# Eight transformer parts on one core: a third of the unweighed scores of the first attention get their log weights from VectorE, and the feed-forwards 1 and 3 are rearranged

## The chip, the cores and the metric

The kernel runs on one core of a Trainium2 chip, as one launch. A core has TensorE (PE: matmul; PEld: its weight loads), VectorE (DVE), ScalarE (ACT), GpSimd (POOL) and SyncE (SP, which issues transfers). Each engine works through its own list of instructions in order, and waits on counting semaphores. The metric is the device time in microseconds, median of some runs.

## The reference

The reference is a chain of eight parts on x of 2 x 1024 tokens with 128 values each; before every part x is normalised (layer norm), and the part's result is added to x. The change touches three places: the scores of the first attention, the first feed-forward and the third one (the parts l0_attn, l0_ffn, l2_ffn of the kernel).

```python
# first attention: 16 heads of 8 values, weight 1/(distance+1) for earlier keys, none for later ones
delta = pos[None, :] - pos[:, None]
log_d = jnp.log(jnp.maximum(delta, 0).astype(jnp.float32) + 1.0)
mask = jnp.where(delta > 0, (-ALPHA * log_d).astype(dtype), jnp.zeros((), dtype))
mask = jnp.where(delta < 0, jnp.asarray(-jnp.inf, dtype), mask)
scores = jnp.einsum('bhqd,bhkd->bhqk', q, k) * scaling
scores = scores + _power_law_mask(S, scores.dtype)[None, None]
attn = jax.nn.softmax(scores, axis=-1)
# first feed-forward: three int32 weights of 384 x 128, times 1/127
h = jax.nn.silu(gate) * up
return jnp.einsum('bsh,dh->bsd', h, wd)
# third feed-forward: 8 experts, each token weighs two of them; every expert is run on all tokens
h = jax.nn.gelu(jnp.einsum('td,edf->etf', xt, w1) + b1[:, None, :], approximate=False)
o = jnp.einsum('etf,efd->etd', h, w2) + b2[:, None, :]
y = _layernorm(xt[None, :, :] + o, ln_g[:, None, :], ln_b[:, None, :])
out = jnp.einsum('et,etd->td', wE, y)
```

## The kernel before

The tokens are 16 tiles of 128, or 4 chunks of 512 (`NC`, `CH`). The parts run one after the other; every engine's list holds all parts, and semaphores join them.

**First attention.** There are 8 units (batch, group of 4 heads). Of each unit 12 groups (512 or fewer queries by 128 keys) are scored; a group has two halves (`p`), and a half is two heads, so there are 192 halves of 2 x 512, 384, 256 or 128 scores. `scores_by_key` (L498 to L524) computes a half into two PSUM banks; the halves' banks go round over three banks (`BANK`), so PE can be one and a half halves ahead, and `free_bank` makes it wait until the bank that it takes next is read. ACT takes the exponential from PSUM to SBUF (`exp`, L606). The weight 1/(distance+1) comes in by one of two ways: for the 133 halves in `BY_POOL`, POOL multiplies the exponentials (`weigh`, L420); for the 59 others PE adds the logarithm to the scores in PSUM, as a high and a low part, by two matmuls with an identity for each head (L518, L519). `times_v` (L540) multiplies by the values up to three groups later. At the same time PE scores the next unit by query in "pieces" (L475, L481, L487), of which DVE takes the row maxima (L671); `split_maxima` (L682 to L690) and `turn_maxima` (L495) make them ready for the next unit, and `divide` (L698, L701) finishes 512 queries. `schedule` writes out one order for all of this, by due positions (one for each half, 24 in a unit), and each engine picks its own steps from it in that order. In unit 0 the pieces come ahead of everything, and unit 7 has none beside it.

**First feed-forward** (`l0_ffn`). For each chunk `wait_xnT` transposes the normalised x on PE (L152) one chunk ahead, ACT copies it to SBUF (L165), PE multiplies it by the gate and the up weights, three times 2 matmuls of 512 columns in float32 (L757), ACT takes silu (L781), DVE multiplies (L795) and so frees the pair of banks (two pairs), and after the next chunk's gates PE multiplies down (`down`, L766). DVE converts the int32 weights (L747) before its last normalisation, and PE waits for that. `add` and `after` on DVE add the result to x (L787) and begin the next norm (L94, L98, L106); POOL computes the reciprocal root (L117, L119).

**Third feed-forward** (`l2_ffn`). There are 8 experts times 4 chunks, 32 steps `n`. In a step PE runs `up(n)` (12 matmuls: w1 and x are split into high and low parts, L1384 to L1386) and `down(n-1)` (L1397, L1402). The weights of expert e+1 are made ready during expert e: ACT rounds w1 to its high part (L1440), POOL subtracts for the low part (L1484) and centres w2 (L1489) with a mean that DVE computes (L1520, L1522). ACT also takes the squares of the sums (L1453), from which POOL computes the scales of each step (L1498, L1500, L1504) for DVE (L1580). The same splitting of x, on ACT (L168) and POOL (L125), is done at the beginning of this part.

## Time and profile before

| what | value |
|---|---|
| median of 3 runs | 1120.84 us (1120.64 to 1128.33) |
| the profiled execution | 1129.11 us, span 1127.3 us |
| mean granted TensorE clock of the span | 0.891 of full speed (full is 2.4 GHz, half is 1.2 GHz) |
| PE busy | 908.3 us, 81% of the span |
| DVE / POOL / ACT busy | 646.1 / 510.8 / 429.1 us |

The busy shares are means over eight parts with different limits, so the parts must be read one by one. The span less the median is 6.5 us: the profiled execution is one of the longer ones.

### The profile page before, as it was taken

How to read it: one execution, taken by the hardware profiler on the slowest of the kernel's cores; microseconds unless marked ns; L12 is line 12 of the kernel's file. 1: busy time of each engine (PE TensorE's matmuls, PEld its weight loads, DVE VectorE, ACT ScalarE, POOL GpSimd, SP SyncE). 2: the span in 40 equal slices, each digit the busy share in tenths (PEclk: the TensorE clock that was granted, in tenths of full speed). 3: DMA queues.
4: the chain of work that ended last, by engine and by line, in shares of the span. 5: the costliest groups of instructions: out<-in, count | busy, mean ns of one | idle time of the engine just before them, and what ended most of it. 6: DMA issues, size and time to landing. Idle time of an engine off the chain costs nothing. (4 is left out here: it accounts for less than half of the span.)

```text
span 1127.3 us, 17905 instructions
## 1 busy us (share of the span) xinstructions
PE 908.3 (81%) x6590; PEld 612.6 (54%) x6590; DVE 646.1 (57%) x1445; ACT 429.1 (38%) x1018; POOL 510.8 (45%) x458
## 2 busy tenths in 40 slices
PE   4558999999998878267899789995998996398983
PEld 2113333333433446154566678885895766388883
DVE  6757676767670155979687556778103666542324
ACT  2324664665556421014111365674344211032221
POOL 4335978897888611052322344554200001156561
PEclk9658999999998988758799599998899998599997
DMA  4800110011000000001000000121100000266664
GB/s 156 238 1 2 29 31 13 18 30 30 3 1 23 1 22 8 0 15 39 1 2 2 10 10 19 46 95 33 43 1 1 1 10 28 77 199 207 201 205 137
DMA packets 38747, 55.95 MB, mean 50 GB/s; under 512 B 6682, under 2 KB 26146, under 8 KB 38534
## 3 DMA queue, kind: packets, MB, share of 16 engines
q1 hardware_dynamic: 36166, 49.70, 14.9%
q0 software_dynamic: 2496, 5.12, 1.4%
q8 instruction: 54, 0.88, 0.3%
q14 instruction: 31, 0.25, 0.1%
HBM read 43.66 MB, written 10.94 MB: 48 GB/s over the span
## 5 line engine op out<-in xcount | busy, mean ns | idle before, releaser
L671 DVE TENSOR_REDUCE arena<-ps 128x2 f32<-128x1024 f32 (+2 forms) x192 | 177.6, 956 | 87.6 <-PE ps L487 55.4
L420 POOL TENSOR_TENSOR arena<-arena 128x1024 f32<-128x1024 f32 (+3 forms) x105 | 201.2, 1957 | 37.9 <-ACT arena L606 37.8
L606 ACT ACTIVATE arena<-ps 128x512 f32<-128x512 f32 (+3 forms) x320 | 138.6, 489 | 89.4 <-PE ps L519 56.2
L117 POOL TENSOR_SCALAR vareps<-meanvar 128x4 f32<-128x4 f32 x32 | 8.0, 251 | 236.2 <-DVE meanvar L98 236.2
L511 PE MATMUL ps<-arena 51*128 51x512 bf16 (+3 forms) x384 | 91.0, 342 | 18.1 <-ACT arena L606 6.8
L511 PEld LDWEIGHTS ps<-arena 51*128 51x128 bf16 x384 | 27.0, 94 | 105.0 <-ACT arena L606 58.6
L2076 PE MATMUL ps<-arena 128*128 128x128 f32 x624 | 78.2, 280 | 0.0
L152 PE MATMUL ps<-ident,xn 128*128 128x128 f32 x128 | 26.4, 356 | 62.1 <-DVE x L922 19.9
L2076 PEld LDWEIGHTS ps<-arena 128*128 128x128 f32 x624 | 74.7, 196 | 0.0
L420 POOL TENSOR_TENSOR xnT<-xnT,arena 128x1024 f32<-128x1024 f32 (+1 forms) x28 | 52.7, 1902 | 40.5 <-ACT xnT L606 40.5
L487 PE MATMUL ps<-arena 48*128 48x512 bf16 (+3 forms) x320 | 56.8, 351 | 16.8 <-DVE arena L671 14.1
L540 PE MATMUL ps<-arena 128*9 128x512 f32 (+3 forms) x640 | 66.6, 492 | 0.0
L2242 DVE TENSOR_TENSOR arena<-ps,arena 128x512 f32<-128x512 f32 x39 | 27.0, 692 | 66.0 <-PE ps L2076 34.7
L1402 PEld LDWEIGHTS ps<-arena 128*128 128x128 f32 x512 | 63.0, 194 | 2.9
L1402 PE MATMUL ps<-arena 128*128 128x128 f32 x512 | 62.9, 276 | 0.0
L165 ACT ACTIVATE xnT<-ps 128x512 f32<-128x512 f32 x32 | 18.9, 596 | 114.3 <-PE ps L152 107.4
L2036 POOL DMA_INDIRECT expert_rows<-arena x39 | 38.6, 990 | 47.6 <-ACT arena L2124 44.5
L152 PEld LDWEIGHTS ps<-ident,xn 128*128 128x128 f32 x128 | 20.0, 186 | 66.0 <-issue 40.7
L2023 POOL DMA_INDIRECT arena<-token_rows,arena x39 | 38.1, 976 | 36.9 <-DVEq L2224 24.7
L1453 ACT ACTIVATE arena<-arena 128x128 f32<-128x128 f32 x128 | 38.0, 298 | 35.8 <-DVE arena L1571 35.8
L1267 DVE TENSOR_TENSOR arena<-ps,arena 128x512 f32<-128x512 f32 x64 | 39.7, 682 | 17.6 <-PE ps L1149 17.6
L2110 ACT ACTIVATE arena<-ps 128x512 f32<-128x512 f32 x39 | 23.3, 597 | 68.1 <-PE ps L2076 58.3
(340 smaller groups left out, 2034.4 us busy)
## 6 DMA issues: line engine op xcount, KB each, us to landing
arena<-in_L_ffn_w SPq DMA_DIRECT2D x39, 512.0 KB
arena<-scratch SPq DMA_DIRECT2D x32, 192.0 KB, 4.0
arena<-in_L_ffn_w SPq DMA_DIRECT2D x16, 256.0 KB, 3.3
scratch<-arena SPq DMA_DIRECT2D x12, 256.0 KB, 4.0
arena<-expert_rows SPq DMA_DIRECT2D x8, 256.0 KB, 4.7
scratch<-arena SPq DMA_DIRECT2D x4, 384.0 KB, 5.7
scratch<-arena SPq DMA_DIRECT2D x12, 128.0 KB, 4.2
x<-in_x SPq DMA_DIRECT2D x4, 256.0 KB, 3.9
```

The costliest lines, as they stand in the source:

```text
L152: last = nc.tensor.transpose(m.ps[:, self.banks[n % len(self.banks)], j * P:(j + 1) * P], m.xn[:, n * TPC + j, :], m.ident[:, :])
L420: nc.gpsimd.tensor_tensor(e, e, weight[:, at:at + k].unsqueeze(1).broadcast_to([P, 2, k]), ALU.mult).then_inc(weighed, 1)
L487: mm = nc.tensor.matmul(m.ps[:, bank + e, 0:wd], qs[rows, u % BUFS, pair, at * P:(at + 1) * P], ks[rows, u % BUFS, pair, j:j + wd], start= ...
L511: mm = nc.tensor.matmul(m.ps[:, bank, 0:wd], ks[rows, u % BUFS, p, kt * P:(kt + 1) * P], qs[rows, u % BUFS, p, CH * qc:CH * qc + wd], star ...
L540: mm = nc.tensor.matmul(m.ps[PAD * h:PAD * h + HD + 1, 7, 0:wd], vones[:, b * TB + kt, u % G * GH + h, :], probs(u * NG + n)[:, h, 0:wd], ...
L606: nc.scalar.activation(probs(g)[:, 2 * p + e, 0:wd], m.ps[:, BANK[h, e], 0:wd], ACT.Exp, scale=SCALE).then_inc(exps, 1)
L671: nc.vector.tensor_reduce(out, scores, AX.X, ALU.max, negate=True).then_inc(max_set, 1)
L1267: nc.vector.tensor_tensor(at[:, t % 2, g, :].rearrange("p (j q) -> p j q", q=P), m.ps[:, g, :].rearrange("p (j q) -> p j q", q=P), causal[ ...
L1402: mm = nc.tensor.matmul(m.ps[:, 4 + n % 2, j * P:(j + 1) * P], hT[:, n % 2, f, j * P:(j + 1) * P], w2c[:, e % 2, f, :], start=False, stop= ...
L2023: nc.gpsimd.indirect_dma_start(xg[:, s % RING, :], None, m.token_rows, bass.IndirectOffsetOnAxis(ap=token_i[:, s:s + 1], axis=0),).then_in ...
L2036: nc.gpsimd.indirect_dma_start(m.expert_rows, bass.IndirectOffsetOnAxis(ap=target_i[:, s:s + 1], axis=0), y[:, s % RING, :], None,).then_i ...
L2076: mm = nc.tensor.matmul(m.ps[:, 2 * (s % 2) + half, f * P:(f + 1) * P], w_up[:, s % WBUFS, at + f * P:at + (f + 1) * P], xgT[:, s % 2, :], ...
```

## The change

- **First attention.** `shares` also picks a third (by columns) of the halves that POOL doesn't weigh, `BY_VECTOR`: 21 halves, of which 8 have 512 columns for each head, 1 has 384, 3 have 256 and 9 have 128. For these PE adds nothing (`with_log` is false); DVE adds the logarithm (`add_logs`) from PSUM into the SBUF buffer of the exponentials, in one instruction where the two banks are neighbours and in two where they aren't, and so frees the banks; ACT then takes the exponential of both heads in place by one instruction (`exp_log`), one position later in the schedule, ahead of the next half's. The 8 wide halves are those of position 8 in each unit.
- **First feed-forward.** x is split into a high and a low part as in the third one (a second copy on ACT, a subtraction on POOL), and the 24 float32 matmuls for gate and up become 48 in float32r. The int32 weights are converted by ACT after the attention's last copy, in two instructions, with the scale moved to silu and to the down weights.
- **Third feed-forward.** Rounding, subtraction, centring and mean of the next expert's weights come at its predecessor's first chunk (`c == 0`) instead of the second; on ACT ahead of the squares and on POOL ahead of the step's scales.
- The second attention's buffers are laid behind the area of the split x, with no other change.

```diff
...
@@ -295,9 +295,14 @@
             if pool + (1500 if diagonal(n) else 0) <= gone:
                 by_pool.add(h)
                 pool += 80 + 2.25 * k
-        return by_pool
-
-    BY_POOL = shares()
+            else:
+                others += k
+                if vector + k / 2 <= others / 3:
+                    by_vector.add(h)
+                    vector += k
+        return by_pool, by_vector
+
+    BY_POOL, BY_VECTOR = shares()
     POOL_COUNT = list(itertools.accumulate(h in BY_POOL for h in range(UNITS * HALVES)))
     def schedule():
@@ -309,7 +314,11 @@
             for n in range(NG):
                 for p in range(2):
                     at = 2 * (u * NG + n) + p
-                    due.setdefault(at, []).append(("exp", u, (n, p)))
+                    if at in BY_VECTOR:
+                        due.setdefault(at, []).append(("log", u, (n, p)))
+                        due.setdefault(at + 1, []).append(("exp_log", u, (n, p)))
+                    else:
+                        due.setdefault(at, []).append(("exp", u, (n, p)))
         for at, pieces in PIECES_AT.items():
             due[at] += [("max", u, n) for u, n in pieces]
         for u in range(UNITS):
...
@@ -342,11 +351,21 @@
             BANK[job] = 4 + k % 3
         freed = {}
         for what, u, n in schedule():
-            h = u * HALVES + 2 * n[0] + n[1] if what == "exp" else None
+            h = u * HALVES + 2 * n[0] + n[1] if what in ("exp", "log", "exp_log") else None
             if what == "exp":
                 for e in range(2):
                     counts[exps] += 1
                     freed[h, e] = (exps, counts[exps])
+                EXPS[h] = counts[exps]
+            if what == "log":
+                for e in range(2):
+                    counts[logged] += 1 if e or BANK[h, 1] != BANK[h, 0] + 1 else 0
+                    freed[h, e] = (logged, counts[logged])
+                if BANK[h, 1] == BANK[h, 0] + 1:
+                    freed[h, 0] = freed[h, 1]
+                LOGGED[h] = counts[logged]
+            if what == "exp_log":
+                counts[exps] += 1
                 EXPS[h] = counts[exps]
             if what == "turn_max":
                 freed[what, u, n] = (mrows_set, u + 1)
@@ -503,7 +522,7 @@
                 pe.wait_ge(mrows_in[u % BUFS], 16 * GH * (u // BUFS + 1))
             wd = width(n)
             with_mask = h in BY_POOL and diagonal(n)
-            with_log = h not in BY_POOL
+            with_log = h not in BY_POOL and h not in BY_VECTOR
             off = weight_at(n)
             for e in range(2):
                 rows = slice(HALF * e, HALF * e + LONG)
...
@@ -605,6 +624,13 @@
                 act.wait_ge(s_mm, 2 * h + e + 1)
                 nc.scalar.activation(probs(g)[:, 2 * p + e, 0:wd], m.ps[:, BANK[h, e], 0:wd], ACT.Exp, scale=SCALE).then_inc(exps, 1)
+        def exp_of_logged(u, at):
+            n, p = at
+            g = u * NG + n
+            ps = probs(g)[:, 2 * p:2 * p + 2, 0:width(n)]
+            act.wait_ge(logged, LOGGED[2 * g + p])
+            nc.scalar.activation(ps, ps, ACT.Exp, scale=SCALE).then_inc(exps, 1)
+
         def take_numerators(u, qc):
             k = u * QC + qc
...
@@ -701,7 +727,25 @@
             nc.vector.tensor_tensor(o[:, t0:t0 + TPC, g * GH * HD:(g + 1) * GH * HD].rearrange("p t (h e) -> p t h e", e=HD),
                                     turned[:, :, :, 0:HD], r.unsqueeze(3).broadcast_to([P, TPC, GH, HD]), ALU.mult).then_inc(o_set, 1)
-        do = {"max": maximum, "split": split_maxima, "divide": divide}
+        def add_logs(u, at):
+            n, p = at
+            g = u * NG + n
+            h = 2 * g + p
+            k = width(n)
+            off = weight_at(n)
+            if g >= RING:
+                dve.wait_ge(pv_mm, g - RING + 1)
+            dve.wait_ge(log_steps, 5)
+            if BANK[h, 1] == BANK[h, 0] + 1:
+                dve.wait_ge(s_mm, 2 * h + 2)
+                nc.vector.tensor_tensor(probs(g)[:, 2 * p:2 * p + 2, 0:k], m.ps[:, BANK[h, 0]:BANK[h, 0] + 2, 0:k],
+                                        logw[:, off:off + k].unsqueeze(1).broadcast_to([P, 2, k]), ALU.add).then_inc(logged, 1)
+            else:
+                for e in range(2):
+                    dve.wait_ge(s_mm, 2 * h + e + 1)
+                    nc.vector.tensor_tensor(probs(g)[:, 2 * p + e, 0:k], m.ps[:, BANK[h, e], 0:k], logw[:, off:off + k], ALU.add).then_inc(logged, 1)
+
+        do = {"max": maximum, "split": split_maxima, "log": add_logs, "divide": divide}
         for what, u, n in schedule():
             if what in do:
                 do[what](u, n)
@@ -726,15 +770,20 @@
 def l0_ffn(nc, m, A, sem, sb, norm):
+
+
     F = 384
     FT = F // P
     SCALE = 1.0 / 127.0
+    m.rounded.fresh()
+    x_high, x_low = norm.split_xnT()
+    w_up = m.rounded.take("l0f_w_up", [P, 2, F], F32R)
     wi = sb("l0f_wi", [P, 3, F], I32)
-    w = sb("l0f_w", [P, 3, F])
+    w_down = sb("l0f_w_down", [P, F])
     sg = sb("l0f_sg", [P, 2, CH])
     hT = sb("l0f_hT", [P, 2, FT, CH])
     w_in, w_all = norm.loads(1)
-    w_scaled = sem("l0f_w_scaled")
+    w_set = sem("l0f_w_set")
     up_done = sem("l0f_up_done")
     sg_done, h_done = sem("l0f_sg_done"), sem("l0f_h_done")
     down_done, x_done = sem("l0f_down_done"), m.x_done
@@ -742,20 +791,23 @@
     def sync(sp):
         sp.dma_start(wi[:, :, :], A["L0_ffn_w"]).then_inc(w_in, 16)
-    def dequantise(dve):
-        dve.wait_ge(w_in, w_all)
-        nc.vector.tensor_scalar(w[:, :, :], wi[:, :, :], SCALE, None, ALU.mult).then_inc(w_scaled, 1)
+    def widen(act):
+        act.wait_ge(w_in, w_all)
+        nc.scalar.activation(w_up[:, :, :], wi[:, 0:2, :], ACT.Copy).then_inc(w_set, 1)
+        nc.scalar.activation(w_down[:, :], wi[:, 2, :], ACT.Copy, scale=SCALE * SCALE).then_inc(w_set, 1)
     def tensor(pe):
         def gates(c):
             norm.wait_xnT(pe, c)
+            cs = slice(c * CH, (c + 1) * CH)
             for f in range(FT):
                 s = c * FT + f
                 if s >= 2:
                     pe.wait_ge(h_done, s - 1)
                 for half in range(2):
-                    nc.tensor.matmul(m.ps[:, 2 * (s % 2) + half, :], w[:, half, f * P:(f + 1) * P], m.xnT[:, c * CH:(c + 1) * CH],
-                                     start=True, stop=True).then_inc(up_done, 1)
+                    out, lhsT = m.ps[:, 2 * (s % 2) + half, :], w_up[:, half, f * P:(f + 1) * P]
+                    nc.tensor.matmul(out, lhsT, x_high[:, cs], start=True, stop=False)
+                    nc.tensor.matmul(out, lhsT, x_low[:, cs], start=False, stop=True).then_inc(up_done, 1)
         def down(c):
             if c >= 2:
...
@@ -778,7 +830,7 @@
         for s in range(NC * FT):
             norm.copy_xnT(act, s // FT + 1)
             act.wait_ge(up_done, 2 * s + 1)
-            nc.scalar.activation(sg[:, s % 2, :], m.ps[:, 2 * (s % 2), :], ACT.Silu).then_inc(sg_done, 1)
+            nc.scalar.activation(sg[:, s % 2, :], m.ps[:, 2 * (s % 2), :], ACT.Silu, scale=SCALE).then_inc(sg_done, 1)
     def vector(dve, after):
         def add(c):
@@ -798,14 +850,14 @@
         add(NC - 1)
     return Part([(x_done, norm.done(c)) for c in range(NC)], tensor=tensor, vector=vector, scalar=scalar, sync=sync,
-                before_norm={"vector": dequantise})
-
+                before_norm={"scalar": widen})
 def l1_attn(nc, m, A, sem, sb, norm):
     H, HD = 16, 8
     HB = NT // 2
     SCALE = HD ** -0.5
+    sb("rounded", [P, 2 * T + 2 * 384])
     wqk = sb("l1a_wqk", [P, 2, D])
     rope = sb("l1a_rope", [P, P])
     w = sb("l1a_w", [P, 5, D])
@@ -1468,12 +1520,12 @@
                 act.wait_ge(step, 2 + RANK_STEPS)
                 nc.scalar.activation(gap[:, :], gap[:, :], ACT.Exp).then_inc(exps, 1)
             if n == 4:
-                for c in range(NC):
-                    turn(c)
+                for k in range(NC):
+                    turn(k)
+            if c == 0 and e + 1 < E:
+                round_weights(e + 1)
             if n:
                 squares(n - 1)
-            if c == 1 and e + 1 < E:
-                round_weights(e + 1)
         squares(STEPS - 1)
     def gpsimd(pool):
@@ -1492,6 +1544,8 @@
         split_weights(0)
         for n in range(STEPS):
             e, c = divmod(n, NC)
+            if c == 0 and e + 1 < E:
+                split_weights(e + 1)
             if n >= 4:
                 pool.wait_ge(y_set, n - 3)
             pool.wait_ge(squared, n + 1)
@@ -1502,8 +1556,6 @@
             if n == 0:
                 pool.wait_ge(wte_set, 1)
             nc.gpsimd.tensor_tensor(wrs[:, n % 4, :], rs[:, n % 4, :], wte[:, c * TPC:(c + 1) * TPC, e], ALU.mult).then_inc(scales, 1)
-            if c == 1 and e + 1 < E:
-                split_weights(e + 1)
     def vector(dve, after):
         count = [0]
@@ -1603,7 +1655,7 @@
                 for k in range(NC):
                     add_biases(k)
                 dve.wait_ge(lnb_added, NC)
-            if c == 1 and e + 1 < E:
+            if c == 0 and e + 1 < E:
                 sum_weights(e + 1)
         for n in (STEPS - 2, STEPS - 1):
             add(n)
```

PE at position 8 of one unit of the first attention, before: the half's scores (L511), its four log matmuls (L518, L519), a piece (L475, L481), and the next half's scores.

```order
L540 MATMUL ps<-xnT,arena 9x512 x4
L511 MATMUL ps<-arena 128x512 x2
L518 MATMUL ps<-rounded 128x512
L519 MATMUL ps<-rounded 128x512
L518 MATMUL ps<-rounded 128x512
L519 MATMUL ps<-rounded 128x512
L475 MATMUL ps<-arena 128x512 x2
L481 MATMUL ps<-arena 128x128 x8
L511 MATMUL ps<-arena 128x512 x2
```

The same place now (L530 are the scores, L494 and L500 the piece):

```order
L559 MATMUL ps<-xnT,arena 9x512 x4
L530 MATMUL ps<-arena 128x512 x2
L494 MATMUL ps<-arena 128x512 x2
L500 MATMUL ps<-arena 128x128 x8
L530 MATMUL ps<-arena 128x512 x2
```

The four log matmuls are gone, so the piece and the next half's scores follow at once. On DVE the same place was, before, a `divide` and then maxima:

```order
L698 RECIPROCAL arena<-ps 128x16 [waits l0a_num_turned]
L701 TENSOR_TENSOR xn<-ps,arena 128x4x32 [waits l0a_rec_set]
L671 TENSOR_REDUCE arena<-ps 128x2x4 [waits l0a_a_mm]
L671 TENSOR_REDUCE arena<-ps 128x2 [waits l0a_a_mm] x6
```

and is now (L746 are the two additions, L697 the maxima):

```order
L724 RECIPROCAL arena<-ps 128x16 [waits l0a_num_turned]
L727 TENSOR_TENSOR xn<-ps,arena 128x4x32 [waits l0a_rec_set]
L746 TENSOR_TENSOR arena<-ps,arena 128x512 [waits l0a_s_mm,l0a_log_steps,l0a_pv_mm]
L746 TENSOR_TENSOR arena<-ps,arena 128x512 [waits l0a_s_mm]
L697 TENSOR_REDUCE arena<-ps 128x2x4 [waits l0a_a_mm]
L697 TENSOR_REDUCE arena<-ps 128x2 [waits l0a_a_mm] x6
```

Two additions stand ahead of the piece's maximum. POOL in the third feed-forward, before: the scales of a step (L1498, L1500, L1504), then the weights of the next expert (L1484, L1489), which stood behind the scales of the second chunk.

```order
L1498 TENSOR_SCALAR arena<-arena 128x4 [waits l2f_squared,l2f_y_set]
L1500 TENSOR_TENSOR arena<-arena,power 128x4 [waits l2f_scales]
L1504 TENSOR_TENSOR arena<-arena 128x4 [waits l2f_scales]
L1484 TENSOR_TENSOR rounded<-arena,rounded 128x256 [waits l2f_up_done,l2f_w1_high_set]
L1489 TENSOR_SCALAR arena<-arena 128x128 [waits l2f_o_done,l2f_w2_summed]
L1489 TENSOR_SCALAR arena<-arena 128x128
```

Now (L1536 and L1541 are the weights, L1552, L1554 and L1558 the scales) they stand ahead of the scales of the first chunk:

```order
L1536 TENSOR_TENSOR rounded<-arena,rounded 128x256 [waits l2f_up_done,l2f_w1_high_set]
L1541 TENSOR_SCALAR arena<-arena 128x128 [waits l2f_o_done,l2f_w2_summed]
L1541 TENSOR_SCALAR arena<-arena 128x128
L1552 TENSOR_SCALAR arena<-arena 128x4 [waits l2f_squared,l2f_y_set]
L1554 TENSOR_TENSOR arena<-arena,power 128x4 [waits l2f_scales]
L1558 TENSOR_TENSOR arena<-arena 128x4 [waits l2f_scales]
```

The block has moved up by the scales of two steps.

## Rows read from the trace of the kernel before

**Rows 1.** Busy time by stretch: us, PE, PEld, DVE, ACT, POOL, clock, DMA.

```profile
72.00:384.00 312.00, 285.93 (x2186) 111.40 (x2187) 186.29 (x238) 178.29 (x406) 251.56 (x132) 0.95 0.06 16
252.00:288.00 36.00, 33.32 (x279) 12.85 (x278) 25.43 (x34) 21.27 (x50) 29.36 (x17) 1.00 0.08 23
402.00:439.00 37.00, 36.52 (x160) 22.90 (x160) 16.83 (x51) 10.84 (x17) 3.21 (x6) 0.92 0.03 6
```

**Rows 2.** Waits in the first attention (80 to 395): us, times, longest.

```profile
PEld ps L511 <- ACT arena L606: 58.6, 126, 0.9
PEld ps L487 <- DVE arena L671: 15.3, 26, 1.4
PEld ps L540 <- POOL arena L420: 0.8, 5, 0.2
```

**Rows 3.** Groups of instructions by shape in the same stretch.

```profile
L606 ACT ACTIVATE arena<-ps 128x512 f32<-128x512 f32 x158 | 84.6, 597 | 43.3 <-PE ps L519 29.9 <-PE ps L511 7.1 <-PE ps L523 6.3
L671 DVE TENSOR_REDUCE arena<-ps 128x2 f32<-128x1024 f32 x55 | 67.1, 1224 | 24.6 <-PE ps L487 24.4
L671 DVE TENSOR_REDUCE arena<-ps 128x2 f32<-128x512 f32 x28 | 19.3, 691 | 10.3 <-PE ps L487 10.3
```

**Rows 4.** Timeline at position 8 of unit 4: start, us, what.

```profile
245.52 4.71 POOL L420 TENSOR_TENSOR arena<-arena 128x1024 f32<-128x1024 f32 x2
246.25 0.29 DVE L701 TENSOR_TENSOR xn<-ps,arena 128x128 f32<-128x128 f32 x1
246.28 0.39 PE L511 MATMUL ps<-arena 51*128 51x512 bf16 x2
246.60 0.50 PE L518 MATMUL ps<-rounded 128*128 128x512 f32 x1
247.63 0.60 PE L475 MATMUL ps<-arena 128*128 128x512 bf16 x2
248.40 0.38 PE L511 MATMUL ps<-arena 51*128 51x512 bf16 x2
249.04 1.08 ACT L606 ACTIVATE arena<-ps 128x512 f32<-128x512 f32 x2 [0.54 <-PE ps L523]
```

**Rows 5.** Timeline at position 14 of unit 5, DVE beside POOL.

```profile
294.28 3.11 DVE L682 TENSOR_TENSOR arena<-arena 128x28 f32<-128x28 f32 x2
294.61 2.52 POOL L420 TENSOR_TENSOR xnT<-xnT,arena 128x512 f32<-128x512 f32 x2
```

**Rows 6.** Timeline of the first feed-forward.

```profile
400.58 1.31 POOL L119 TENSOR_TENSOR rstd<-vareps,power 128x4 f32<-128x4 f32 x1
401.90 1.97 PE L152 MATMUL ps<-ident,xn 128*128 128x128 f32 x8 [5.80 <-DVE arena L747]
403.70 7.50 PE L757 MATMUL ps<-xnT,arena 128*128 128x512 f32 x12
411.48 5.32 PE L757 MATMUL ps<-xnT,arena 128*128 128x512 f32 x12
416.63 2.84 PE L766 MATMUL ps<-arena 128*128 128x128 f32 x24
```

**Rows 7.** Groups that split x, at the beginning of the third feed-forward.

```profile
L125 POOL TENSOR_TENSOR rounded<-xnT,rounded 128x512 fp32r<-128x512 f32 x4 | 5.2, 1305 | 6.4 <-ACT rounded L168 6.4
L168 ACT ACTIVATE rounded<-xnT 128x512 fp32r<-128x512 f32 x4 | 2.5, 630 | 0.1
```

**Rows 8.** Third feed-forward: its wait, and the timeline at a new expert.

```profile
PEld ps L1384 <- POOL rounded L1484: 9.7, 6, 2.1
704.11 0.48 PE L1384 MATMUL ps<-rounded 128*128 128x512 f32 x1
707.51 0.48 PE L1384 MATMUL ps<-rounded 128*128 128x512 f32 x1
712.48 0.50 PE L1384 MATMUL ps<-rounded 128*128 128x512 f32 x1 [1.33 <-POOL rounded L1484]
711.70 0.73 POOL L1484 TENSOR_TENSOR rounded<-arena,rounded 128x256 fp32r<-128x256 f32 x1
```

16 lines of the change are left out of this document (8 added, 8 removed).

## The prediction

> **What bounds the kernel now.** I read the busy times by stretch first. In the first attention PE is busy 285.93 of 312 us, POOL 251.56, DVE 186.29 and ACT 178.29; in its middle PE is busy 33.32 of 36 us at full clock [rows 1]. So PE comes first, POOL has about a fifth to spare, DVE two fifths. The waits say what PE's rest is: it waits for ACT to read a bank, 126 times and 58.6 us by the weight loads, never over 0.9 us; it waits for DVE's maxima 26 times, 15.3 us; for POOL's weighing 0.8 us [rows 2]. That is a PE with a short leash: three banks let it run one and a half halves ahead of the exponentials. Work taken from PE is therefore a gain only as far as ACT and the banks keep up. In the first feed-forward PE is busy 36.52 of 37 us [rows 1], so it is the bound alone. In the third, the wait to look at is that of an expert's first matmul for POOL's low part of the weights: six times, 9.7 us, 2.1 at most [rows 8].
>
> **First attention.** For 21 of 59 halves the log matmuls go. At 512 columns the four of them hold PE from 246.60 to 247.63, 1.03 us [rows 4]. The 21 halves have 8 x 512 + 384 + 3 x 256 + 9 x 128 = 6400 columns a head; by columns that is 6400 / 512 x 1.03 = 12.9 us of PE, the most that this part can give (a little more, since narrow ones have a fixed share).
>
> What it adds is DVE's. No row has an addition of a PSUM tile and an SBUF row of this size; the maximum of 512 columns from PSUM takes 691 ns and of 1024 takes 1224 [rows 3], and I take the same: 6400 x 2 / 1024 x 1.22 = 15 us, some 17 with the fixed parts. DVE goes from 186 to 203 of 312 and stays no bound. What counts is latency. I walk through position 8, which is in each unit and has 512 columns. The scores start at 246.28 and are there 0.39 later, at 246.67; DVE has finished with L701 at 246.54 [rows 4] and is free. Its additions end near 247.4 and 248.1 (the order shows two of them, each frees its bank). PE does the piece at once: it took from 247.63 to 248.40, 0.77 us [rows 4], so the next scores could start at 246.60 + 0.77 = 247.4 instead of 248.40. So far a gain of 1.0. But ACT now waits for 248.1, and then takes both heads in one instruction, about 1.05 us (two of 597 ns [rows 3], less one start), to 249.15. Before, it began the next half at 249.04 [rows 4]. So ACT gains nothing, and PE two halves on needs a bank that ACT reads until 249.15 + 0.6 = 249.75. Before, PE got there at 249.04 + 1.08 = 250.1 or a little later, as the half's second exponential was done. What is left is 0.4 to 0.5 of the 1.0. I take 0.5 for each of the 8 wide halves: 4 us.
>
> Of the 13 narrower halves PE loses at least 2304 / 512 x 1.03 = 4.6 us of work. Some stand at positions 22 and 23, right after a maximum that DVE is still at, and two at position 15, behind `split_maxima`, whose first two instructions took 3.11 us there [rows 5]: the additions queue behind it, then ACT's exponential of that half, and behind that its next one, while PE has to wait for the same maxima anyway. One at position 14 of unit 0 goes the other way: `split_maxima` stands behind the additions and so waits for scores that it did not need. I take plus 1.5 for those that lie well and minus 1.5 for these: nothing. Sum for the attention: 4 us. Ends: 13 if PE stays the bound everywhere; 4 us slower if each of the 21 costs a maximum's length on ACT's path (1.22) where PE is given 0.6 to 1.03.
>
> POOL's work is the same; at 251.56 of some 308 it is still not the bound. Its first instructions of a unit run back to back, but the multiplication by v comes three groups later, and the 0.8 us in [rows 2] say how seldom that is late.
>
> **A rule of the skill on DVE's additions.** While POOL ran without a pause (245.52 to 250.23), DVE's L701, one input from PSUM and one from SBUF, took 0.29 us [rows 4]. DVE's L682, both inputs in SBUF and only 28 columns, took 3.11 us for two, and ended with POOL's two instructions (297.39 against 297.13) [rows 5]. The Trainium skill (SBUF — State Buffer, section "SBUF: two separate sides") says that POOL and a VectorE instruction with two SBUF inputs take a shared pair of ports as an exclusive lock; by that rule the additions, with one input in PSUM, are free of it, and the trace agrees. It is the rival below if it is otherwise.
>
> **First feed-forward.** At the beginning PE no longer waits for the int32 conversion (5.80 us idle, released by L747) [rows 6]. But its first gates now wait for the first x_low. POOL is at the reciprocal roots until 400.58 + 1.31 = 401.89 [rows 6], and a subtraction takes 1.305 [rows 7]: 403.2, against 403.70 [rows 6]. Gain 0.5. The two conversions on ACT lie in its idle time ahead of this. The gates of the first chunk took 7.50 us, mostly at half clock; the next chunk's took 5.15 (411.48 to 416.63) [rows 6]. A float32r matmul costs 1.03 / 4 = 0.26 [rows 4], 12 for a chunk 3.1; at half clock up to 6.2, by most of the chunk at half clock 5.7. First chunk: gain 0.5 + 1.8 = 2.3. The other three: 5.15 - 3.1 = 2.05 each, less a new stall. Two pairs of banks: the third product waits for DVE's multiplication of the first, 1.03 + 0.60 + 0.69 + signals = 2.4 after the start, where PE could start it at 2.06; and while a chunk is being copied ahead, ACT does two copies of 0.60 and 0.63 [rows 3, 7] before its first silu. That is 0.3 to 1.3 a chunk; I take 1.0. Gain 3 x 1.05 + 2.3 = 5.4; I take 5. The down matmuls (2.84) [rows 6] stay and give the chain time. Ends: 2, if the stall takes all of the 2.05; 9, if there is none.
>
> **Third feed-forward.** A step takes 707.51 - 704.11 = 3.40 us, but that into a new expert 712.48 - 707.51 = 4.97 [rows 8]: 1.57 more, and POOL's L1484, from 711.70 for 0.73, releases it. Five such and one of 2.1 are the 9.7. The block moves up by the scales of two steps, 6.8 us, against a lateness of 1.6; L1484 then ends some 5 us before PE wants it. What is late next? Its inputs: ACT rounds after the first chunk's gelus, three steps ahead. DVE's mean comes two steps before the need. The block on POOL, 2.0 us, now stands in front of the first chunk's scales, for which POOL also waits until DVE has the mean; DVE uses these scales two steps later, so I put it at 0.2 in all. The next load from DRAM starts earlier too, and is waited for nowhere. Gain 9.5; ends 8 and 10.
>
> **Sum.** 4 + 5 + 9.5 = 18.5 us. The profiled execution has 1129.1 (a span of 1127.3 and 1.8 around it) and would have 1110.6. It is 8.3 above the median of the runs shown, and nothing of the sum hangs on that; against the median, 1120.8 - 18.5 = 1102.3.
>
> **Rivals.**
> - *PE is the bound throughout the attention.* The 33.32 of 36 speaks for it, the 126 waits for ACT against. 13 instead of 4: 1093.
> - *The attention gives nothing.* DVE's additions come late behind maxima, ACT's list stands still behind them, and the banks stay full: the leash decides. For it: the 58.6 us of waits. With 0 to 3 us lost there and 2 to 5 in the first feed-forward: 1120.8 - 9.5 - 3.5 + 1.5 = 1109.
> - *The clock falls.* PE's mean clock over the stage is 0.95 [rows 1]. Another 5% of it at half clock, 16 us, would cost up to 8: 1110. Against it: the middle of the stage has many short waits already and runs at 1.00 [rows 1]. The Trainium skill (TensorE: Matmul & The Clock Gate, section "A second HAM failure mode: psum-queue depth-cycling") warns that frequent short idle times while PE cycles through banks make the clock change between its levels; the trace doesn't show that here.
> - *The additions are held up by POOL*, as L682 was. Then each of the 21 halves waits for one POOL instruction at least, 4.71 / 2 = 2.36 [rows 4], and ACT, the banks and PE behind it: 50 us, 1120.8 + 50 - 14.5 = 1156. It decides from 0.9 us a half on (14.5 + 4 over 21). L701 speaks against it.
>
> **How the numbers follow.** Forecast 0.55 (its own range 1097 to 1107), PE bound 0.12, nothing from the attention 0.22, clock 0.07, held up 0.04. A measurement of this kernel can tell about 1% from no change, 11 us: 1109.6. The forecast, the PE case, most of the third and half of the clock's lie below it: 0.83 faster, 0.13 the same, 0.04 slower. The range runs from the PE case to the clock's: 1091 to 1112.
>
> **What the profile will show.** PE's wait for L1484's successor gone, and the 32 steps 3.40 us apart (if not: the third part of the sum is wrong). Additions of 0.69 or 1.22 us while POOL is busy (if 2 or more: held up). ACT waiting for DVE at its exponentials in place, and PE's waits for ACT grown while its log matmuls shrink by 84; the stage near 308 us. In the first feed-forward 48 matmuls 0.26 apart, PE idle about 1 us a chunk, and the part 5 us shorter. Wrong would be, above all, an attention that is no shorter, or gains in it over 8 us.

## The result

The changed kernel takes 1116.7 us, the median of 20 runs (1107.9 to 1122.2). The kernel before, run beside it, takes 1127.3 (20 runs, 1120.0 to 1131.7), not the 1120.8 of the three runs shown before. The ratio is 0.991, with a 95% interval of 0.989 to 0.993: 10.6 us faster, where 18.5 were forecast. The means of the experiments below take in all runs; without those that took over 1.5% longer than the fastest of their kernel (three of e6, one of e8, three of e11), these three kernels stand 3.1, 23.4 and 23.9 us below the kernel before instead of -0.1, 21.6 and 18.2, and no reading below hangs on the difference.

From the two profiles I took the times at which the stages begin and end (first scores of the first attention, its last addition to x, first matmul of the second attention that reads x, first matmul with w1 of the third feed-forward, its last addition to x).

| stage | before | after | forecast |
|---|---|---|---|
| first attention | 325.9 | 333.9 | -4 |
| from there to the second attention | 48.2 | 41.5 | -5 |
| second attention and what follows | 194.0 | 194.1 | 0 |
| third feed-forward | 143.3 | 133.7 | -9.5 |
| from there to the end, not edited | 343.0 | 339.2 | 0 |

The two feed-forwards gave 6.7 and 9.6 us, as forecast; the attention, for which a gain of 4 was forecast, lost 8.0. Its busy times, and the lines of the same view around one place in unit 4 (the columns are those of [rows 1]):

```profile
72.00:384.00 312.00, 279.53 (x2074) 98.75 (x2074) 204.35 (x271) 173.57 (x376) 247.26 (x129) 0.92 0.06 16
...
254.40:257.60 3.20, 2.98 (x30) 0.96 (x26) 3.17 (x2) 0.89 (x4) 3.20 (x4) 1.00 0.00 0
257.60:260.70 3.10, 1.41 (x18) 0.75 (x14) 2.59 (x7) 0.68 (x1) 0.34 (x1) 1.00 0.00 0
260.70:264.10 3.40, 3.40 (x24) 0.91 (x22) 2.24 (x2) 2.37 (x5) 2.04 (x1) 0.50 0.04 10
```

DVE went from 186.29 us to 204.35, as forecast (203). But the granted clock of the stage fell from 0.95 to 0.92. The last three lines show such a fall: PE is busy 2.98 of 3.20 us at full clock (2.4 GHz), then only 1.41 of 3.10, and the next 3.40 us are granted at 0.50 (1.2 GHz). The stage (to its last addition) has 59.0 us at the half clock, against 29.0 before. Two of the stage's falls, at 260.7 and at 342.6, begin 1.3 and 2.3 us behind the end of a gap of over 1.1 us in which PE waits for the same line; two more such gaps, ending at 221.73 and 300.08, have no fall within 11 us. The timeline shows whose the gap at 259.37 is:

```profile
254.54 3.64 DVE L708 TENSOR_TENSOR arena<-arena 128x28 f32<-128x28 f32 x2
255.31 1.26 POOL L439 TENSOR_TENSOR xnT<-xnT,arena 128x512 f32<-128x512 f32 x1
256.53 1.41 POOL L439 TENSOR_TENSOR arena<-arena 128x256 f32<-128x256 f32 x2
259.02 0.30 DVE L716 TENSOR_TENSOR arena<-arena 128x32 bf16<-128x32 f32 x1
259.37 0.61 PE L514 MATMUL ps<-arena 128*12 128x128 bf16 x8 [1.69 <-DVE arena L716]
260.02 1.01 ACT L645 ACTIVATE arena<-ps 12x1024 bf16<-12x1024 bf16 x1 [3.59 <-PE ps L514]
```

`split_maxima` (L708, 28 columns, both inputs in SBUF) starts at 254.54 and its two instructions end at 258.2, just after POOL's weighing has stopped at 257.94. PE waits for the end of the split to turn the maxima. The groups by shape say what such an instruction takes on average, and what an addition takes:

```profile
L708 DVE TENSOR_TENSOR arena<-arena 128x28 f32<-128x28 f32 x7 | 16.4, 2349 | 0.2
L746 DVE TENSOR_TENSOR arena<-ps,arena 128x512 f32<-128x512 f32 x16 | 10.3, 686 | 3.4 <-PE ps L530 3.4
```

The additions take 0.69 us, as the maxima of the same width do [rows 3], while POOL runs. The Trainium skill (SBUF — State Buffer, section "SBUF: two separate sides") says that POOL and a VectorE instruction with two SBUF inputs exclude each other; the trace agrees for both kinds.

The waits of the same stretch:

```profile
PEld ps L530 <- ACT arena L625: 55.7, 114, 1.5
...
ACT arena L632 <- DVE arena L746: 27.3, 12, 4.0
...
PEld ps L514 <- DVE arena L716: 13.1, 7, 2.6
```

PE's wait for ACT is what it was (58.6 us, 126 times [rows 2]), though 84 log matmuls are gone; ACT now waits for additions, up to 4 us; and PE waits longer for the split's last line than it did in the kernel before:

```profile
PEld ps L495 <- DVE arena L690: 8.9, 6, 2.5
```

In the first feed-forward the gates start 4.14 us after the last addition to x (405.95) instead of 4.84:

```profile
408.68 2.49 POOL L125 TENSOR_TENSOR rounded<-xnT,rounded 128x512 fp32r<-128x512 f32 x2
408.74 3.03 DVE L106 TENSOR_SCALAR xn<-x,meanvar,rstd 128x128 f32<-128x128 f32 x4 [0.47 <-POOL rstd L119]
410.09 0.76 PE L809 MATMUL ps<-rounded 128*128 128x512 f32 x1 [2.98 <-POOL rounded L125]
414.87 0.60 PE L152 MATMUL ps<-ident,xn 128*128 128x128 f32 x4
415.23 0.48 PE L809 MATMUL ps<-rounded 128*128 128x512 f32 x1
419.14 2.84 PE L818 MATMUL ps<-arena 128*128 128x128 f32 x24
```

The first chunk's gates take 5.14 us (410.09 to 415.23), mostly at half clock, where 7.78 were taken (403.70 to 411.48 [rows 6]); the second chunk's take 3.91 (to 419.14) instead of 5.15. In the third feed-forward the steps into experts 3 to 7 are 3.40 us apart like those around them, and no wait for POOL's low part (now L1536) is left; only among the first nine steps are there longer ones, up to 10.70 us, as before (10.15):

```profile
701.48 0.48 PE L1436 MATMUL ps<-rounded 128*128 128x512 f32 x1
702.27 0.74 POOL L1536 TENSOR_TENSOR rounded<-arena,rounded 128x256 fp32r<-128x256 f32 x1
704.88 0.48 PE L1436 MATMUL ps<-rounded 128*128 128x512 f32 x1
```

### The profile page after: what moved, and what is told of

It is laid out like the page before. It is cut to its first block and busy times, and to the rows that moved or that the text cites. A ratio compares the mean times of both kernels' runs of the same rounds, so it can differ in the third digit from the quotient of the medians.

```text
span 1114.5 us, 17760 instructions
## 1 busy us (share of the span) xinstructions
PE 898.0 (81%) x6506; PEld 603.8 (54%) x6506; DVE 666.1 (60%) x1477; ACT 429.0 (38%) x1003; POOL 511.9 (46%) x462
## 5 line engine op out<-in xcount | busy, mean ns | idle before, releaser
L697 DVE TENSOR_REDUCE arena<-ps 128x2 f32<-128x1024 f32 (+2 forms) x192 | 177.3, 954 | 69.4 <-PE ps L506 49.7
L625 ACT ACTIVATE arena<-ps 128x512 f32<-128x512 f32 (+3 forms) x278 | 122.8, 499 | 58.3 <-PE ps L538 29.4
L530 PE MATMUL ps<-arena 51*128 51x512 bf16 (+3 forms) x384 | 96.2, 352 | 23.4 <-ACT arena L625 8.7
L530 PEld LDWEIGHTS ps<-arena 51*128 51x128 bf16 x384 | 28.2, 95 | 118.9 <-ACT arena L625 56.0
L559 PE MATMUL ps<-arena 128*9 128x512 f32 (+3 forms) x640 | 73.8, 540 | 0.0
L2088 POOL DMA_INDIRECT expert_rows<-arena x39 | 38.5, 987 | 41.2 <-ACT arena L2176 40.6
L152 PEld LDWEIGHTS ps<-ident,xn 128*128 128x128 f32 x128 | 18.9, 177 | 63.6 <-issue 43.3
```

The lines of the kernel that those rows point to most:

```text
L152: last = nc.tensor.transpose(m.ps[:, self.banks[n % len(self.banks)], j * P:(j + 1) * P], m.xn[:, n * TPC + j, :], m.ident[:, :])
L530: mm = nc.tensor.matmul(m.ps[:, bank, 0:wd], ks[rows, u % BUFS, p, kt * P:(kt + 1) * P], qs[rows, u % BUFS, p, CH * qc:CH * qc + wd], star ...
L559: mm = nc.tensor.matmul(m.ps[PAD * h:PAD * h + HD + 1, 7, 0:wd], vones[:, b * TB + kt, u % G * GH + h, :], probs(u * NG + n)[:, h, 0:wd], ...
L625: nc.scalar.activation(probs(g)[:, 2 * p + e, 0:wd], m.ps[:, BANK[h, e], 0:wd], ACT.Exp, scale=SCALE).then_inc(exps, 1)
L697: nc.vector.tensor_reduce(out, scores, AX.X, ALU.max, negate=True).then_inc(max_set, 1)
L2088: nc.gpsimd.indirect_dma_start(m.expert_rows, bass.IndirectOffsetOnAxis(ap=target_i[:, s:s + 1], axis=0), y[:, s % RING, :], None,).then_i ...
```

## The experiments

Three theories stand behind the expectations. **L** (the lock): `split_maxima` is held up by POOL, and the additions make that worse. **C** (the clock): with its log matmuls gone TensorE has too little to do, and its clock is taken down. **B** (banks and ACT's order): the additions hold banks, and ACT's list stands still behind them.

The runs are in three groups (e1 to e4, e5 to e8, e9 to e12), each on one chip with the kernel before beside them; before took 1127.1, 1133.9 and 1132.3 us (medians of 16 or 17). So kernels of different groups are compared by their distance to before, in means of all their runs; differences are taken before rounding. The changed kernel's own 20 runs are a fourth group, in which before's clock is known for the profiled run only; 0.894 is taken for it. "Clock" is the mean granted clock of these whole runs (before: 0.894, 0.891, 0.894). Within a kernel, the runs with a lower clock are the longer ones: over all 157 runs, with a level of its own for each kernel and group, by 6.8 us for each 0.01. "At one clock" is the distance with both sides brought to 0.890 by that slope. It is an estimate: taken kernel by kernel, the slope lies anywhere from 1.8 to 10.5 us. "Attention" is the profiled stage, with its half-clock time.

| kernel | log matmuls of the 21 halves | DVE's additions | POOL's wait | less than before, us | clock | at one clock | attention (half clock) |
|---|---|---|---|---|---|---|---|
| before | yes | no | no | 0 | 0.894 | 0 | 325.9 (29.0) |
| changed | no | yes | no | 10.2 | 0.878 | 21.2 | 333.9 (59.0) |
| e1, attention alone | no | yes | no | -4.9 | 0.884 | 2.3 | 334.9 (62.0) |
| e2, feed-forwards alone | yes | no | no | 19.0 | 0.891 | 21.1 | 332.3 (45.6) |
| e3 | no | yes | yes | 18.0 | 0.878 | 28.9 | 327.2 (65.8) |
| e4 | yes | no | yes | 25.7 | 0.894 | 25.9 | 318.5 (21.5) |
| e12, e4 again | yes | no | yes | 26.3 | 0.895 | 25.9 | 324.6 (38.5) |
| e5 | dead, ahead | yes | yes | 14.1 | 0.893 | 12.6 | 332.0 (28.4) |
| e6 | dead, ahead | yes | no | -0.1 | 0.878 | 8.9 | 344.9 (61.9) |
| e7 | all but at position 8 | at position 8 | yes | 24.3 | 0.888 | 26.5 | 320.1 (34.4) |
| e8 | at position 8 | elsewhere | yes | 21.6 | 0.883 | 27.2 | 324.7 (48.6) |
| e9 | no; as much dead work with V, behind | yes | yes | 2.9 | 0.886 | 8.6 | 343.6 (53.5) |
| e10 | no | no, unweighed | yes | 36.8 | 0.890 | 39.5 | 311.1 (38.3) |
| e11 | all but at 8 to 15 | at 8 to 15 | yes | 18.2 | 0.882 | 26.5 | 317.2 (27.4) |

**e1 and e2: the two parts of the change apart.** e1 is the kernel before with the attention's part of the diff, e2 with the feed-forwards' parts.

> The kernel before with the attention's part of the change alone. My prediction's sum had 4 us of gain for it. What the profile after suggests instead is a loss: from the first scores to the last addition to x it is 8 us longer. Theory L (the shared lock): the additions lie ahead of the maxima on DVE and shift DVE against POOL, so that the first instruction of the split of the maxima (both inputs in SBUF) starts where POOL works without a pause, and is held longer; PE stands for it once a unit. Theory C (the clock): PE has 84 matmuls fewer, stands more often, and falls to half clock. Theory B (banks and ACT's order alone): ACT waits for the additions. All three expect 3 to 10 us slower than before here. L expects the mean of the 28-column instruction over 2 us (1.57 before); C more than 30 us at half clock in the stage (10 before); B ACT's waits for the additions to end PE's waits, with no change in the split.

> The kernel before with the changes of the first and third feed-forward alone, the attention as before. My sum had 5 + 9.5 = 14.5 us; the profile after shows 6.7 + 9.6 = 16. If the parts add up, 15 to 17 us faster than before, and faster than the changed kernel by 4 to 8. If the attention's part is worth the 4 us that I forecast and something else is wrong, this kernel is slower than the changed one.

e1: 1131.1 us, ratio 1.004 (1.002 to 1.006). e2: 1109.2, ratio 0.984 (0.981 to 0.988). The attention's part alone makes the kernel slower, by 4 to 5 us; put upon e2 it costs 8.8 (19.0 to 10.2). The feed-forwards give 19.0, more than the 15 to 17 expected: the third gained 12.4 us in e2's profile, 9.6 in the changed kernel's. (The "10 before" of half clock in the expectation of e1 leaves out the start of the stage; the whole stage has the 29.0 of the table.)

**e3 and e4: POOL pauses for the split.** POOL waits once a unit, before its first weighing from position 12 on, for the split of the next unit's maxima; e3 is the changed kernel with it, e4 is e2 with it.

```
+    if u + 1 < UNITS and waited == u and 2 * n + p >= 12:
+        pool.wait_ge(nparts_set, u + 2)
+        waited = u + 1
```

> The changed kernel, but POOL waits once in each unit, ahead of its first weighing from position 12 on, until DVE has split the maxima (a wait for nparts_set). Nothing is left out. Theory L: DVE's first split instruction is no longer held, its mean falls from 2.35 us to under 0.8, PE's wait for the split (13.1 us in seven units) falls to under 6, and the kernel is 4 to 10 us faster than the changed one; POOL has the time, since it pauses for 3 us right after. Theory C alone: half clock as often, time within 2 us of the changed kernel. Theory B: no gain, or a loss from POOL's later weighing.

> The kernel with the two feed-forward changes and the attention as before, with the same wait of POOL for the split of the maxima. Theory L: the split was held before the change too (1.57 us in the mean for 28 columns), so this gains 2 to 6 us over the kernel without the wait, and is the fastest of the four. If the lock isn't what holds it, no change, or slower by POOL's pause.

e3: 1108.0, ratio 0.985 (0.982 to 0.988). e4: 1100.5, ratio 0.978 (0.975 to 0.981), faster than both kernels. The split's first instruction, in e3, e4 and e2 in this order:

```profile
L712 DVE TENSOR_TENSOR arena<-arena 128x28 f32<-128x28 f32 x7 | 4.3, 621 | 0.2
```
```profile
L686 DVE TENSOR_TENSOR arena<-arena 128x28 f32<-128x28 f32 x7 | 3.3, 477 | 0.2
```
```profile
L682 DVE TENSOR_TENSOR arena<-arena 128x28 f32<-128x28 f32 x7 | 15.4, 2201 | 0.2
```

That the split waits for POOL is real and is worth 7 us, but it is worth nearly as much without the additions (19.0 to 25.7, 6.7 us) as with them (10.2 to 18.0, 7.8). It is an old cost of this kernel (1574 ns in the profile of before) and not what the change lost. Theory L falls as the cause. With the split free, the additions still cost 7.7 us.

**e5, e6 and e9: TensorE gets its work back.** If the loss is that TensorE has too little to do and its clock is taken down, dead work must bring it back. In e5 and e6 the four log matmuls are issued ahead of the half's scores, which start the sums anew, so that what is computed stays the same. In e9 the matmuls against V of each added half are issued twice more, behind the group's; its keys are so counted three times, and what e9 computes is not the reference.

```
+                if h in BY_VECTOR:                      # e5, e6: ahead of the half's scores
+                    bank = free_bank((h, e))
...
+                    nc.tensor.matmul(m.ps[:, bank, 0:wd], identr, log_high[:, off:off + wd], start=True, stop=False, ...)
+                    nc.tensor.matmul(m.ps[:, bank, 0:wd], identr, log_low[:, off:off + wd], start=False, stop=True, ...)
...
+            heads = list(range(GH)) + [2 * p + e for p in range(2) if ... in BY_VECTOR for e in (0, 1, 0, 1)]   # e9
```

> The kernel of e3 (the changed one with POOL's wait), in which each half added by VectorE also issues its four log matmuls again, ahead of its scores, into the same two banks; the scores' matmuls then start the sums anew, so the four are dead work and what is computed is unchanged. TensorE has the work of the kernel before, VectorE and ACT have that of the changed one. Theory C (the clock): e3 lost 9 us of attention to e4 (327.2 against 318.5 us) because its TensorE, with less to do, ran 66 us at the half clock against 22. With the work put back the half-clock stretches of positions 20 to 23 go, the attention takes 318 to 321 us and the kernel 1100 to 1102 us. Theory B (banks and ACT's order): the additions and the late exp are what cost, they are all still there: attention near 327 us, kernel 1107 to 1110 us, half-clock time near 60 us.

> The changed kernel with the same dead log matmuls ahead of the scores of the halves that VectorE adds, and without POOL's wait. With e5, the changed kernel and e3 it makes a table of two by two: POOL's wait or not, dead work or not. Theory C with L (the shared lock): the dead work takes away the half-clock stretches that follow from thin work and leaves those that follow from the split being held up; attention 325 to 330 us (333.9 in the changed kernel), kernel 1107 to 1112 us; the split's first instruction stays near 2.3 us. Theory B: no gain, 1115 to 1119 us.

> The kernel of e3 again with TensorE's work put back, this time where no bank and no addition waits for it: behind a group's matmuls against V, those of the two heads of each half that VectorE adds are issued twice more (four matmuls of the half's width, as many columns as its log matmuls had). The keys of these halves are so counted three times over in numerators and denominators. In e5 the dead work stood ahead of the scores and of VectorE's addition, so it made their chain longer by 4 matmuls, 1.1 us at each position 8, and that hid what the clock gave back (half-clock time fell from 66 to 28 us). Theory C (the clock): with the work behind, half-clock time again falls to 20 to 35 us; the attention takes 317 to 322 us against e3's 327.2; against the kernel before on the same chip -22 to -26 us, where e3 had -18. Theory B (banks, ACT's order): attention stays at 326 to 330 us, -14 to -18 us, since nothing of the additions changed and TensorE got more to do.

e5: 1118.2, ratio 0.988 (0.984 to 0.993). e6: 1132.3, 0.997 (0.994 to 1.001). e9: 1130.7, 0.998 (0.995 to 1.001). No theory had these times. In e5 the clock came back as C said (0.878 to 0.893 over the run, 65.8 to 28.4 us of half clock in the attention), yet the kernel got 3.8 us slower; in e9 the clock came back in part (0.886) and 15 us were lost. At one clock the dead work costs 16.3 us in e5 and 20.3 in e9 (28.9 less 12.6 and 8.6); its columns are 12.9 us of TensorE. So work on TensorE is paid for in full in this stage, though TensorE also waits in it, and the clock gives back less. e6 is 14.2 us behind e5 (11.0 without its three longest runs): without POOL's wait, there too, the kernel is slower, and its clock is as low (0.878) as that of the changed kernel, though TensorE's work is back.

**e7, e8 and e11: only some of the halves.** One line after `shares()` keeps the halves with position 8, those without, or those below 16.

```
+        by_vector = {h for h in by_vector if h % HALVES == 8}      # e7; != 8 in e8; < 16 in e11
```

> The kernel of e3, but of the 21 halves that VectorE adds only the eight at position 8 of each unit (512 and 256 wide heads of the unit's wide groups) stay; the 13 others go back to log matmuls on TensorE. The half-clock stretches of e3 began at positions 20 to 23 and none at positions 8 to 15. Theory C: the stretches go, each unit's positions 8 to 15 keep 0.4 to 0.7 us of gain against e4, attention 313 to 316 us, kernel 1095 to 1098 us, the fastest so far. Theory B: an addition at position 8 delays ACT's list as any other does, attention 318 to 322 us, kernel 1100 to 1104 us.

> The kernel of e3, but the eight halves at position 8 go back to log matmuls, and the 13 at positions 14 to 23 stay with VectorE. Theory C: the half-clock stretches at the ends of units stay (50 to 66 us in the attention), attention 326 to 330 us, kernel 1107 to 1111 us, no faster than e3. Theory B: the loss of e3 against e4 (9 us of attention for 21 halves) is spread over the additions, 13 of them cost 5 to 6 us: attention 323 to 325 us, kernel 1104 to 1106 us.

> The kernel of e3, of whose 21 halves only the eleven at positions 8 to 15 are added by VectorE (position 8 of every unit, 14 or 15 of three). In e3 and e7 these thirds of a unit ran at full clock and were 0.2 to 1.0 us shorter than in e4. Theory C: attention 313 to 317 us, 2 to 4 us less than in e4 on the same chip, kernel 1 to 4 us below e4, unless TensorE's thinner work starts half-clock stretches in the thirds behind (e7 had 34 us of half clock, e4 21.5). Theory B: 1 to 4 us above e4.

e7: 1110.5, ratio 0.980 (0.976 to 0.984). e8: 1113.0, 0.983 (0.978 to 0.987). e11: 1116.0, 0.987 (0.984 to 0.991); its runs spread from 1101.3 at a clock of 0.897 to 1120.3 at 0.872. None is faster than e4; the intervals of e7 and e8 overlap those of e4 and e12, e11's lies above them. C's forecast that e7 would be the fastest was wrong, and so was its forecast that e8 would be no faster than e3. B's forecasts fit both: 320.1 us of attention in e7 (318 to 322) and 324.7 in e8 (323 to 325), and 24.3 and 21.6 us less than before, where B had 23 to 27 and 21 to 23. e11's attention (317.2) is as C had it, its time isn't.

**e10: the log matmuls left out, nothing in their place.** e4, in which the 21 halves' scores are exponentiated unweighed, so that this part of the mask is missing.

```
-            with_log = h not in BY_POOL
+            with_log = h not in BY_POOL and h not in BY_VECTOR
```

> The kernel of e4 (all log weights by TensorE, POOL's wait), in which the log matmuls of the 21 halves are left out and nothing takes their place: these halves' scores are exponentiated unweighed, so that part of the mask is missing. VectorE and ACT do exactly what they do in e4, TensorE has as little as in e3. Theory C: the half-clock stretches of e3 come back though there is no addition: 45 to 70 us of half clock in the attention (e4: 21.5, e3: 65.8), attention 318 to 326 us, no better than e4 or worse, kernel within 4 us of e4 or slower. Theory B: without additions there is nothing that could cost; half-clock time stays at 20 to 30 us and the attention falls by 21 times 0.4 to 0.85 us to 303 to 311 us, the kernel 8 us or more below e4.

> The kernel of e4 again, on the chip of these runs, as the measure for e9 to e11: in call and chip of e4 it was 26 us faster than the kernel before (ratio 0.978). Both theories expect 24 to 27 us again and 318 to 321 us of attention; if it differs by more than that, the differences of 2 to 4 us between e4, e7 and e8, which ran on different chips, mean nothing.

e10: 1095.1, ratio 0.968 (0.965 to 0.972). e12: 1105.2, 0.978 (0.975 to 0.981), as e4 had it. e10 decides. Taking the log matmuls from TensorE gives 10.6 us (26.3 to 36.8), 13.6 at one clock, near the 12.9 that the prediction named as the most that this part can give, and costs little clock (0.895 to 0.890). So thin work alone isn't what takes the clock down, and C as it was stated falls. What costs is the additions: e3 has the same matmuls as e10 and is 18.9 us slower (18.0 against 36.8). Of these 10.6 are left at one clock (39.5 less 28.9): that is B, the latency of VectorE in front of ACT and the banks. The other 8.3 come with the clock, 0.890 to 0.878; how the 18.9 part into these two hangs on the slope, the sum doesn't. With TensorE's work alike, the additions bring the clock down. They don't do it in every kernel: in e5, with dead matmuls ahead of them, the clock is that of before (0.893 to 0.891), and in e6, without POOL's wait, it is not (0.878). The busy times of 72 to 380 us, in e3, e10 and e12:

```profile
72.00:380.00 308.00, 282.45 (x2095) 100.92 (x2093) 190.91 (x271) 175.56 (x382) 251.61 (x131) 0.90 0.07 16
```
```profile
72.00:380.00 308.00, 280.72 (x2179) 105.77 (x2180) 184.80 (x264) 180.78 (x412) 254.74 (x137) 0.94 0.07 16
```
```profile
72.00:380.00 308.00, 287.27 (x2180) 111.86 (x2178) 173.77 (x238) 177.68 (x404) 250.78 (x131) 0.94 0.07 16
```

The same clock without the log matmuls as with them, 0.94, and 0.90 with the additions; e4, the same code as e12, has 0.96 in this stretch. Where a fall begins, one place shows. The end of unit 1 in e3, where positions 22 and 23 are DVE's, in the timeline, and then by stretch:

```profile
152.10 0.96 DVE L701 TENSOR_REDUCE arena<-ps 128x2 f32<-128x768 f32 x1 [1.00 <-PE ps L510]
152.32 0.44 PE L534 MATMUL ps<-arena 51*128 51x128 bf16 x3
152.97 0.41 DVE L745 TENSOR_TENSOR arena<-ps,arena 128x256 f32<-128x256 f32 x1
153.42 0.42 ACT L636 ACTIVATE arena<-arena 128x256 f32<-128x256 f32 x1 [0.36 <-DVE arena L745]
153.44 0.23 PE L534 MATMUL ps<-arena 51*128 51x128 bf16 x1 [0.68 <-DVE arena L745]
```

```profile
149.40:152.80 3.40, 3.10 (x32) 1.13 (x31) 1.93 (x2) 2.35 (x7) 3.40 (x3) 1.00 0.00 0
152.80:154.40 1.60, 0.96 (x7) 0.53 (x7) 1.18 (x4) 0.81 (x3) 1.60 (x2) 0.99 0.00 0
154.40:161.20 6.80, 6.69 (x32) 1.09 (x31) 3.73 (x6) 2.90 (x7) 3.62 (x3) 0.50 0.48 118
```

The same place in e10, in the same two views:

```profile
151.13 0.44 PE L520 MATMUL ps<-arena 51*128 51x128 bf16 x3
151.46 0.45 ACT L615 ACTIVATE arena<-ps 128x128 f32<-128x128 f32 x2 [0.16 <-PE ps L520]
151.79 0.23 PE L520 MATMUL ps<-arena 51*128 51x128 bf16 x1 [0.21 <-ACT arena L615]
```

```profile
151.60:156.70 5.10, 4.28 (x35) 1.20 (x35) 3.55 (x6) 3.20 (x9) 3.18 (x3) 1.00 0.67 157
```

In e3 the bank of the next scores belongs to an addition, which stands behind a maximum on DVE (152.10 to 153.06) and ends at 153.38: PE stands still for 0.68 us, and from 154.4 on it runs 6.8 us at the half clock. In e10 ACT frees the bank, PE waits 0.21 us, and the clock stays. Gaps of 0.68 and 0.70 us for the same L745 end at 304.36 and 374.56 in e3, ahead of 10.2 us each at the half clock from 304.6 and 376.2. The Trainium skill (TensorE: Matmul & The Clock Gate, section "A second HAM failure mode: psum-queue depth-cycling") has frequent short idle times of PE cycling through banks as a cause of such falls; these three places agree with it. Others don't: the same gap of 0.68 us ends at 192.72 in e3 with no half clock before 229.5; in e8, which keeps these additions, the gap at the end of unit 1 ends at 154.80 and those behind it at 192.12, 305.26 and 373.20, and only the last has a fall within 3 us (376.0). So such a gap is neither enough for a fall nor, by the falls of e4, e10 and e12, needed for one, and no run here changed one alone.

**What a stretch takes at full clock.** From the start times of the scores I took the length of each third of each unit (positions 0 to 7, 8 to 15, 16 to 23). Wherever a third has no half-clock time in e4 and in e12, which are the same code, its length is the same within 0.02 us, so that with POOL's wait the effects can be read apart (without it they can't: 8 to 15 of units 1 and 3, at full clock, differ by 0.36 and 0.44 us between before and e2, whose attention is the same):

| third | e4 and e12 | e3 | e10 |
|---|---|---|---|
| unit 1, 8 to 15 (position 8 DVE's) | 13.92 | 13.45 | 12.93 |
| unit 4, 8 to 15 (position 8 DVE's) | 13.53 | 13.06 | 12.54 |
| unit 2, 16 to 23 (22 and 23 DVE's) | 12.12 | 11.51 | 11.33 |
| unit 0, 16 to 23 (21 DVE's) | 11.71 | 11.02 | 10.93 |
| unit 6, 16 to 23 (22 DVE's) | 10.81 | 10.90 | 10.23 |
| unit 2, 0 to 7, 5.0 us of it at half clock in e3 | 11.78 | 13.38 | 11.78 |

At full clock, with POOL's wait, the change gains 0.47 us at position 8, and 0.6 to 0.7 at the ends of units 0 and 2, and so, in other kernels with these additions, at those of units 1 and 3. The eleven thirds that are at full clock in e3 as well as in e4 or e12 give 5.1 us together. The table's last line is the price of the half clock: 1.6 us for 5.0. Another one, unit 6's end in e2, took 14.37 with 9.6 us of half clock instead of 10.81. That is 0.32 to 0.37 us for each us of half clock; the slope over whole runs says 0.30 (6.8 us for 0.01, which is 22 us of half clock in 1120). By 0.33 the 17.0 us that the attention of e12 has more than that of e4, the same code, make 324.1 of 318.5; it measured 324.6 (318 to 321 had been expected).

## Why the prediction was wrong

- **The step that failed is the attention's term, "Sum for the attention: 4 us".** Alone (e1) that part measured 4.9 us of loss, and upon e2 8.8. Its walk through position 8 was right where the split is not held up: 0.5 forecast, 0.47 measured at full clock in e3. e10 shows 0.99 where no addition stands in the way, so the other half does go to ACT's wait for DVE. But in the changed kernel the split is held up, and the 0.5 is mostly lost before the third ends: at full clock, 8 to 15 of units 1, 3 and 5 are within 0.05 us of e2's and that of unit 4 is 0.70 us longer. The narrow halves were put at nothing: some gained 0.6 to 0.7 a unit end, some lost (unit 6, 0.09). At one clock, by the slope, the whole of it is 3.0 us of gain with POOL's wait (25.9 to 28.9; the thirds at full clock say 5.1 or more) and about nothing without (21.1 to 21.2), against 4 forecast. What was missing above all is the clock as a term of the sum. It stood among the rivals at 0.07, with 16 us more of half clock; over the whole run it was (0.8936 - 0.8778) x 2 x 1105 = 35 us from e4 to e3 and 29 from e2 to the changed kernel, by the slope 10.7 and 8.9 us: more than all the gain. The term's lower end, 4 us slower, was mis-sized too: 1.22 against 1.03 makes 4 for 21 halves, but with the 0.6 that it gave for the narrow ones it is 9.6.
- **Its argument against that rival failed too.** I read that the middle of the stage "has many short waits already and runs at 1.00". It does, but it isn't where the additions stand behind a maximum on DVE while a bank is theirs. At the units' ends the groups are narrow, a gap of 0.7 us stands among short matmuls, and behind three of them in e3 stretches at half clock began. I had named positions 22 and 23 and the maximum in front of them, and priced only the delay.
- **Additions held up by POOL:** right that they are not (686 ns). But the same lock acts upon `split_maxima`, whose rows I quoted [rows 5] and took as a price only for what queues behind it. It holds up the turning of the maxima, and costs about 7 us with and without the change (e2 to e4, changed to e3): a gain that lay open in the profile of before.
- **First feed-forward:** 5 forecast (2 to 9), 6.7 measured: 0.7 at the beginning (0.5 forecast), 2.6 in the first chunk (1.8), 1.2 in the second and as much in the third (1.05).
- **Third feed-forward:** 9.5 forecast, 9.6 measured in the changed kernel, and 10 to 13 in the other kernels with this part. The wait is gone and the steps are even from the ninth on, as said of all 32.
- **The level.** 1102 was set against a median of three runs, 1120.8; twenty runs gave 1127.3, and the profiled execution (1129.1) was nearer to that. This moves the forecast by 6.5 us, as much as the error of the sum (8). Against 1127.3 the forecast would have been 1108.8, inside the range, with 1116.7 outside of it all the same.

**What stays open:** which gaps bring the clock down, and what the additions cost by themselves and what ACT's exponential one position later: the two came together in every run. The gaps of 0.68 us for a bank stand ahead of three of e3's stretches, and such gaps stand elsewhere with nothing behind them; other stretches (from 229.5, 267.0 and 348.9) have only waits of the usual kind before them, and e12 has 10.2 us each from 266.7 and 352.1, where e4, the same code, has 3.4 us from 350.4 alone. And e7, e8 and e11 do not say which halves are the costly ones: at one clock all three stand with e4 (26.5, 27.2 and 26.5 against 25.9), and what they lose by the clock (0.888, 0.883, 0.882) has no order that follows from the positions. That the additions lower the clock, where the log matmuls are gone, is measured (e3 beside e10); that they do it by the gaps at the banks is not shown: of the eight such gaps of e3 and e8, four have a fall within 3 us behind them and four have none.

## What to carry to other kernels

Where the matmul engine runs with few banks, work that is moved to another engine's in-order queue brings that queue's delays to the banks. Before such a move, look at what stands in front of the new instruction on its queue at each place, and price the gap it makes on PE twice, once as time and once as the stretch of half clock that may follow. An experiment that only leaves the work out, beside one that moves it, tells the gain from the cost at once; here they were 10.6 us gained and 18.9 lost.

A small VectorE instruction with both inputs in SBUF, beside a POOL that runs without a pause, is worth a look in any profile: a pause of POOL at the right place gave 7 us for three lines.
